# Shorter lags between the stages of an edge stream, other route bounds, and a later load of the second expert

## What is computed

```
hn  = layernorm(x)
z   = hn @ W_func.T ;  h_s = hn @ W_self.T
e   = leaky_relu([z[src], z[dst], edge_attr] @ W_att.T)
a   = softmax of e over the edges of one target
x   = x + hn + relu(h_s + segment_sum(a * z[src], dst))     # hn where a node has no edge
y   = layernorm(x)
p   = softmax(y @ router_w.T);  keep the 2 largest of 8, scaled to sum 1
out = x + sum over the two experts of p_e * (silu(y @ w1_e.T) * (y @ w3_e.T)) @ w2_e.T
```

## Time and profile before

| | us |
|---|---|
| median of 3 runs | 1053.97 |
| the three runs | 1053.77 to 1055.1 |
| the profiled execution, its own time | 1052.19 |
| its span, from the first to the last instruction | 1050.0 |
| PE busy / DVE / POOL / ACT in the span | 849.4 / 635.3 / 590.1 / 449.5 |
| gathers of the stream, first and last start | 51.6 and 573.7 |
| marker behind the last logits | 621.92 |

### The profile page before, as it was taken

How to read it: one execution, slowest core, us unless ns; L and a number is a source line. 1 busy time by engine, 2 the same in 40 slices (tenths; PEclk the granted TensorE clock), 3 DMA queues, 4 the chain that set the end, 5 groups by cost and what they waited for, 6 DMA issues and landing times.

```text
span 1050.0 us, 19071 instructions
## 1 busy us (share of the span) xinstructions
PE 849.4 (81%) x4512; PEld 707.3 (67%) x4513; DVE 635.3 (61%) x2235; ACT 449.5 (43%) x1066; POOL 590.1 (56%) x554
## 2 busy tenths in 40 slices
PE   6954888964776777677577968999999999999995
PEld 6811444654664566465456856998988989898994
DVE  6624555565655677766677858556556555656553
ACT  4422233454556546545645861343424333342331
POOL 1077777777777777777776003635455353535332
PEclk9986998988888789788878979999999999999998
DMA  7676576556555455555555243544243522222221
GB/s 235 209 229 207 179 214 183 142 138 220 137 146 143 134 147 138 139 146 135 143 148 135 68 130 129 126 83 101 58 109 60 111 34 41 36 40 35 41 41 20
DMA packets 81158, 128.86 MB, mean 123 GB/s; under 512 B 21373, under 2 KB 56706, under 8 KB 80594
## 3 DMA queue, kind: packets, MB, share of 16 engines
q0 software_dynamic: 30720, 69.90, 28.6%
q1 hardware_dynamic: 43161, 51.59, 16.1%
q10 hardware_dynamic: 7200, 6.56, 1.9%
HBM read 106.86 MB, written 17.86 MB: 119 GB/s over the span
## 4 chain that ended last, share of the span: by engine, by line
PE 56%; DVE 12%; issue 10%; DMA 9%; POOL 7%; DVEq 3%; ACT 1%; POOLq 0%; SPq 0%; ACTq 0%
PE bank L1439 17%; PE bank L1373 13%; DMA early<-ztab,early 7%; PE bank L1480 7%; POOL early L828 7%; PE bank L1334 3%; PE bank L1487 3%; PE bank L1468 3%; PE bank L1160 2%; DVE acc L1906 2%; PE bank L1176 1%; PE bank L1245 1%; PE bank L1242 1%; PE bank L1213 1%; DVE early L1849 1%
## 5 line engine op out<-in xcount | busy, mean ns | idle before, releaser
L828 POOL DMA_INDIRECT early<-ztab,early x416 | 396.7, 954 | 174.6 <-issue 171.8
L1439 PE MATMUL bank<-split_w,operands 128*128 x1344 | 235.4, 324 | 3.8 <-issue 2.7
L1373 PE MATMUL bank<-early,W 128*128 128x258 f32 x832 | 231.7, 430 | 4.9 <-DVE W L1883 4.6
L1439 PEld LDWEIGHTS bank<-split_w,operands 128*128 128x128 f32 x1344 | 211.0, 189 | 9.1 <-issue 7.6
L1373 PEld LDWEIGHTS bank<-early,W 128*128 128x128 f32 x832 | 170.7, 215 | 53.1 <-issue 23.2
L875 POOL DMA_INDIRECT xg<-ttab,slot_rows x56 | 58.3, 1040 | 235.5 <-DVE late L2075 163.7
L1049 ACT ACTIVATE W<-early 128x128 f32<-128x128 f32 x208 | 91.0, 484 | 124.5 <-PE bank L1373 121.3
L1334 PE MATMUL bank<-ident,early 128*16 128x128 f32 x104 | 24.4, 382 | 137.5 <-DVE early L1866 137.4
L868 POOL DMA_INDIRECT out_rows<-late,slot_rows x56 | 103.1, 1841 | 36.6 <-issue 15.4
L1129 ACT ACTIVATE late<-bank 128x384 f32<-128x384 f32 x56 | 27.4, 490 | 198.7 <-PE bank L1439 193.7
L1334 PEld LDWEIGHTS bank<-ident,early 128*16 128x16 f32 x104 | 10.4, 121 | 149.5 <-DVE early L1866 146.8
(11 more groups left out here) (243 smaller groups left out, 1415.6 us busy)
## 6 DMA issues: line engine op xcount, KB each, us to landing
W<-in_wt SPq DMA_DIRECT2D x26, 512.0 KB, 4.5
W<-in_experts SPq DMA_DIRECT2D x40, 266.5 KB, 2.8
early<-ztab,early POOLq DMA_INDIRECT x416, 2.9
W<-in_experts SPq DMA_DIRECT2D x3, 2132.0 KB, 9.0
early<-in_x SPq DMA_DIRECT2D x26, 128.0 KB, 2.2
early<-ztab SPq DMA_DIRECT2D x25, 128.0 KB
early<-late SPq DMA_DIRECT2D x25, 128.0 KB
out_rows<-early ACTq DMA_DIRECT2D x25, 128.0 KB, 2.1
```

The costliest lines, as they stand in the source:

```text
L828: nc.gpsimd.indirect_dma_start(out=zg[:, k * KG + c, :], out_offset=None, in_=ztab, in_offset=bass.IndirectOffsetOnAxis(ap=src_here[:, k / ...
L1373: last = mm(ps[2 + k // 2 % 2][:, 0:ZR], prob_hot[:, k % 3, c * P:(c + 1) * P], zg[:, k * KG + c, :], start=(k % 2 == 0 and c == 0), stop= ...
L1439: last = mm(bank[:, 0:n], x[:, (k % 2 * KC + c) * P:(k % 2 * KC + c + 1) * P], split_w[:, bass.ds(at + (part + w + c * H), n)], start=(i = ...
```

## The change

The lags of the lists are made smaller and the stages inside a step stand in another order. Sums (`weighted`) go from lag 8 to 6, `spread` from 7 to 6, `exps`, `largest` and `shifted_down` from 7 to 5, `runs` and `runs_T` from 5 to 4, `back_copy`, `mirror_back` and `distance` from 6 to 5, `add_sums` from 9 to 7. A tile's path starts at lag 18 instead of 21 (`settled_den`) and ends at lag 25 instead of 34 (`logit_copy` and the routes). `node_load` goes from lag 25 to 18 on SP. The waits that guard shared banks follow (`BEHIND`, `hi + 6`, `ROUTES[b][1] + 6`), as do the steps in which PE runs filler products (`BUSY_FROM`). The middle route takes 9 tiles and the last one 8. SP waits for the marker instead of the last sums before it loads expert 1.

```
-BEHIND = SETTLED // BATCH + 2
+BEHIND = SETTLED // BATCH + 1
-ROUTES = ((0, 8), (8, 16), (16, TILES))
+ROUTES = ((0, 8), (8, 17), (17, TILES))
...
-                                                 (SETTLED + 13, tiled(node_load))])
-                sp.wait_ge(sums_added, GROUPS // 2)
-                sp.wait_ge(next_added, GROUPS // 2)
+                                                 (SETTLED + 6, tiled(node_load))])
+                sp.wait_ge(stream_over, 1)
                 expert_load(1)
...
-                run(act, GROUPS, AHEAD, PEEL, [(7, exps), (7, spread), (6, back_copy), (6, distance), (0, later_scores),
+                run(act, GROUPS, AHEAD, PEEL, [(5, back_copy), (SETTLED + 11, tiled(std2)), (SETTLED + 7, tiled(share_of)),
...
-                run(pe, GROUPS, AHEAD, PEEL, [(4, score_rows_of), (8, weighted), (6, mirror_back),
+                run(pe, GROUPS, AHEAD, PEEL, [(5, mirror_back), (SETTLED + 12, tiled(hn2_T)),
+                                              (6, weighted), (SETTLED + 7, tiled(share_behind)),
...
-                run(dve, GROUPS, AHEAD, PEEL, [(5, runs), (7, largest), (0, plus_s1), (7, shifted_down), (9, add_sums),
+                run(dve, GROUPS, AHEAD, PEEL, [(6, spread_rest), (SETTLED + 13, tiled(logit_copy)), (0, plus_s1),
```

More of the change, by code:

```diff
@@ L83 @@
 EXPERTS_AFTER = (44,)
-BUSY_FROM, BUSY_TO = GROUPS - SETTLED - 7, GROUPS - SETTLED + 2
+BUSY_FROM, BUSY_TO = GROUPS - SETTLED - 6, GROUPS - SETTLED + 2
 LAST_AT = BATCH * (TILES - 2) + 1
@@ L1355, in mirror_back @@
                     for b, (lo, hi) in enumerate(ROUTES[:-1]):
-                        if batch(k, r) == hi + 8:
+                        if batch(k, r) == hi + 6:
                             pe.wait_ge(choice_ready, 3 * b + 3)
@@ L1818, in later_scores @@
                     for part in range(1, len(PARTS)):
-                        if isinstance(t, int) and t == COPY_AT[part] + 3:
+                        if isinstance(t, int) and t == COPY_AT[part] + 2:
                             scores_kept(part)
@@ L1915, in settled_den @@
                     den_of(j, k, r)
-                run(dve, GROUPS, AHEAD, PEEL, [(5, runs), (7, largest), (0, plus_s1), (7, shifted_down), (9, add_sums),
-                                               (0, s2_at), (SETTLED + 9, tiled(settled_den)),
-                                               (SETTLED + 14, tiled(where_edge)), (0, s2_sum),
-                                               (SETTLED + 13, tiled(x_plus_hn)), (SETTLED + 14, tiled(residual)),
-                                               (0, plus_s2), (SETTLED + 15, tiled(stats2)), (SETTLED + 17, tiled(inv_std2)),
-                                               (0, leaky), (SETTLED + 15, tiled(mean_var2)),
-                                               (SETTLED + 17, tiled(neg_mean2)), (SETTLED + 22, tiled(logit_copy)),
-                                               (7, spread_rest), (0, later_scores), (SETTLED + 22, route)])
+                run(dve, GROUPS, AHEAD, PEEL, [(6, spread_rest), (SETTLED + 13, tiled(logit_copy)), (0, plus_s1),
+                                               (5, largest), (7, add_sums), (0, s2_at), (5, shifted_down),
+                                               (SETTLED + 6, tiled(settled_den)), (SETTLED + 10, tiled(where_edge)),
+                                               (SETTLED + 11, tiled(inv_std2)), (0, s2_sum), (SETTLED + 8, tiled(x_plus_hn)),
+                                               (SETTLED + 10, tiled(residual)), (SETTLED + 11, tiled(neg_mean2)),
+                                               (0, plus_s2), (SETTLED + 10, tiled(stats2)), (0, leaky),
+                                               (SETTLED + 10, tiled(mean_var2)), (4, runs), (0, later_scores),
+                                               (SETTLED + 13, route)])
                 v.memset(tick[:, :], 0.0).then_inc(stream_over, 1)
```

16 lines of the change are left out of this document (7 added, 9 removed).

## The result

The changed kernel takes 1064.37 us (median of 4 runs, 1062.32 to 1066.92) beside 1054.53 for the kernel before: a ratio of 1.0101, 95% interval 1.0087 to 1.0115. It is slower by about 1%, and the forecast of 1052.6 with its range up to 1056.0 was wrong. Its profiled execution took 1064.42 us with a span of 1062.3, that is 12.3 over the span of before.

A forecast was written before the change was run, and what follows sets the result against it. The prediction took POOL's gather issues to bound the stream, followed by a drain to the marker. Marker 0.4 us earlier and 1.0 less behind it sum to -1.4, on the median 1053.97: 1052.6, range 1048.5 to 1056.0.

The forecast's parts named there:

- The stream: The 104 groups of gathers: POOL waits for nobody, 5.03 us a group, so shorter lags gain and cost nothing there.
- the slower rival: PE at half clock through most of the drain, marker behind 624, kernel over 2.1 us slower; chance 0.13.
- starving ring: Rival in the stream: waits within longer steps starve the ring and POOL stalls, +5 us, 1058; chance 0.04.
- The drain: From the stream's end to the marker: marker at 617.9 at full clock, 4.0 us below 621.92.
- link (a): Drain's start: group 103's score, sums of 98, score rows to 584.5, then scan and one-hots of 99 to 587.5.
- the three of the prediction: Places in the drain where PE is mostly idle: 584.5 to 587.5, 593.2 to 595.3 and 603.8 to 609.
- link (d): Drain's end: tiles 22 to 24 in turn through one bank, from 603.8 to 617.9.
- Link (b): Drain after 587.5: sums of 99, tile 21, statistics, root, one-hots of 101 to 595.3; PE hole of 2.2 us.
- PE's clock: In the drain: two falls to half clock, +1.0 and +2.6 us, moving the marker from 617.9 to 621.5.
- Group 103: The last group, at the drain's start: VectorE takes it up at 578.4, 1.2 us late (bounds 0 and 2.2).
- The table of the exponential: ACT's table load in the drain, between back-copy and exponential: 1.28 us, ends before it matters, adds 0.
- Behind the marker: Last route has 16 pairs of one-hots instead of 18 and fewer columns: -1.0 us; expert 1's later load adds 0.

The follow-up runs named there:

- e6: Kernel before with only the routes' split changed, to 8, 9 and 8 tiles: 1055.13 us, ratio 1.0001.
- e10: Kernel before with 8 filler matmuls a step instead of 2 in its last steps: 1056.38 us, ratio 1.0013.
- e4: Changed kernel with VectorE's one-hots of groups written as scalar_tensor_tensor instead of tensor_scalar, order as it is: 1073.05 us, ratio 1.0176.
- e1: Changed kernel with VectorE's one-hots of groups moved to mid-step, behind add_sums: 1096.76 us, ratio 1.0425.
- e13: e9 with further PE fillers ahead of the two clock falls still left in the drain: 1052.72 us, ratio 0.9993.
- e5: Changed kernel with VectorE's scan moved on into the next step, behind the one-hots and the logits' copy: 1057.4 us, ratio 1.0024.
- e14: e13 with 3 instead of 8 fillers a step in the last steps: 1053.28 us, ratio 0.9992.
- e7: e5 plus filler matmuls on PE in the drain, no list changed: 1055.21 us, ratio 1.0000.
- e2: Changed kernel with VectorE's one-hots of groups back ahead of the scan, lag 5 for 6: 1055.76 us, ratio 1.0021.
- e3: Kernel before with VectorE's one-hots of groups moved directly behind the scan, lag 8 for 7: 1069.52 us, ratio 1.0155.
- e8: e5 with ScalarE's one-hots of groups ahead of the tile's root, share and idle: 1056.09 us, ratio 1.0007.
- e9: e5 with both ScalarE's one-hots ahead of the root and the PE fillers in the drain: 1054.31 us, ratio 0.9992.
- e11: Changed kernel with VectorE's one-hots of groups using two fixed numbers instead of per-partition scalars: 1063.9 us (2 runs), ratio 1.009.
- e12: Changed kernel with the scan replaced by one tensor_tensor maximum of the same operands: 1055.62 us, ratio 1.0018.

## Why the prediction was wrong, step by step

**The stream: wrong, and this is the step that failed.** "So the stream of 104 groups lasts as long as POOL issues, 5.03 us a group, and the change leaves POOL's order alone." POOL's order is left alone, and the stream does last as long as POOL issues; but that is 5.13 us a group now, for a gather's own duration is not fixed. I took 1.26 us from issue to issue for a property of POOL, asked only whom POOL waits for the earlier trace rows, and priced the reordering of VectorE's list at 0. A wait that lies inside an instruction is shown by no row of waits; it is shown by that instruction's longest duration. The fault can be named more narrowly: I followed what waits on VectorE's moved one-hots ("sums behind VectorE's one-hots of the same step"), and not what they stand next to. The order of the two lists showed the new neighbours. The size: 9.5 us in the profiles; by the ratios 1.0101 - 1.0024 is about 8 us. (In e6 and e10, whose lists are those of before, the last gather starts at 575.4 and 575.2, so some 1.5 us of such a difference can be scatter.) Of the signs that were named, the first one caught it, the last gather at 573.7. The sign of the slower rival, a marker behind 624, came too, and misled: most of the marker's lateness was there before the drain began.

A page of the Trainium skill speaks to it that I didn't weigh: "SBUF — State Buffer", section "Who interferes with whom". It says that VectorE and GpSimd share one pair of ports, that GpSimd needs it to generate the descriptors of its own DMAs, and that a VectorE instruction in a two-port mode, which tensor_scalar can enter, blocks GpSimd for the whole of it where it issues first. The trace agrees in kind: nine gathers of 1.65 to 2.08 us beside such instructions. It differs in the condition. The same tensor_scalar apart from the scan (80 times in that stream) never has a gather of over 1.18 us beside it, and the other form, with two tensors as its inputs, which by the page interferes with an instruction of GpSimd that reads, holds the gathers at least as long (e4). By that rule alone, without what stands ahead of the one-hots, the kernel before would hold gathers too: its 95 pairs of one-hots in the stream have no gather over 1.09 beside them.

**No wait of POOL, no starving ring: right** in the changed kernel (its gaps are 0.30 throughout). e1 shows what the rival would have looked like.

**The drain: partly right in form, too short in size.** At full clock the sum ran from the last gather at 573.7 to 617.9, 44.2 us. e13, at full clock but with fillers in PE's way, took 48.7. How long the drain is at full clock without them no run shows. Up to the end of tile 22's products the sum gave 30.1 from the last gather's start (573.7 to 603.8) and e13 needs 32.4 (575.10 to 607.55). In link (a) I let PE have the sums of 98 as soon as their one-hots are there, and overlooked the sums of 97 ahead of them: in e5 PE stands still for 2.72 us, a hole that isn't among the three of the prediction, runs the sums of 97 at half clock (3.58) and comes to those of 98 9.2 us behind the last gather, for the 7.0 of the sum. The score rows end 12.4 behind it, for 10.8. In link (d), 14.1 of the sum, e13 needs 16.3 and e14, with fewer late fillers, 15.2. Link (b) was right: its hole of PE, predicted at 2.2, is 2.34, behind the predicted chain of root, share, idle, one-hots:

```profile
605.62 0.29 ACT L966 ACTIVATE early<-early,eps 128x1 f32<-128x1 f32 x1 [2.43 <-DVE early L1644]
...
606.62 0.86 ACT L1048 ACTIVATE W<-early 128x128 f32<-128x128 f32 x2
...
607.53 2.72 PE L1371 MATMUL bank<-early,W 128*128 128x258 f32 x7 [2.34 <-ACT W L1048]
```

**PE's clock: the right worry, set too low.** Two falls for 3.6 us were forecast. The changed kernel's windows show it below full speed in most of the drain:

```profile
595.00:600.00 5.00, 2.93 (x11) 2.36 (x12) 2.12 (x6) 2.91 (x7) 0.00 (x0) 0.80 0.00 0
605.00:610.00 5.00, 2.66 (x8) 2.03 (x8) 1.47 (x7) 3.71 (x10) 0.00 (x0) 0.82 0.29 89
620.00:625.00 5.00, 4.07 (x18) 3.23 (x19) 0.66 (x3) 2.06 (x6) 0.00 (x0) 0.69 0.15 52
630.00:635.00 5.00, 3.39 (x18) 2.39 (x18) 1.44 (x9) 3.56 (x6) 0.00 (x0) 0.71 0.24 80
```

From 595 to 635 the windows lie between 0.69 and 1.00; in the drain before they were at 1.00 up to the fall at 618. e7 prices it: about 2.5 us, just clear of the intervals. The slower rival, half clock through most of the drain, names a part of the loss, but not the larger one. The page that the prediction set beside it, "TensorE: Matmul & The Clock Gate" of the Trainium skill, section "HAM oscillation — how this bites in real kernels", tells of matmuls that run at the low level again and again behind waits. The traces agree: behind a hole of 2.72 eight sum rows take 3.58 us in e5, and with that hole filled 1.98 in e13.

**Group 103:** predicted 4.7 us after the last gather's start. It was 5.6 in the changed kernel and 4.7 in e5 (580.46). Right to within a microsecond, once the stream is set aside (5.4 in e13).

**The table of the exponential:** predicted 0. The exponential starts 0.01 to 0.02 behind the load's end, as in the earlier trace rows; VectorE does wait for it, 1.98 us once, but PE has other sums in that time. Right for what the runs can tell.

**Behind the marker:** predicted -1.0, found -0.4 in the profiles, and e6, the routes alone, gives no gain that can be measured. Expert 1 is as predicted: its conversions begin 8.4 us behind the marker (9.4 predicted), and the copy of the tokens stands at 650.45, 15.8 behind it (15.4 predicted), waiting for PE and not for the conversions:

```profile
643.08 3.85 ACT L549 ACTIVATE split_w<-W 128x2842 fp32r<-128x2842 f32 x2 [3.82 <-DMA W<-in_experts]
650.45 0.38 ACT L1004 ACTIVATE acc<-bank 100x256 f16<-100x256 f32 x1 [3.53 <-PE bank L1295]
```

**The sum of it.** Predicted -1.4, by the median of the runs about +10. Of this the pair of scan and one-hots is about 8 us (shown by e2, e5 and, the other way round, e3). The other 2.5 are the drain: PE's holes and the half clock behind them. Fillers alone give them back (e7); ScalarE's one-hots ahead of the root gain 1.8 (e8), which isn't clear of noise. In no run do the shorter lags themselves gain anything measurable in the drain: with these losses taken away (e9, e13) the kernel is level with the kernel before. As e13's fillers cost PE time of their own, a gain without them isn't excluded.

## What to carry to other kernels

An engine that waits for nobody is still not independent: before a reordering is priced at nothing, look at the longest duration of the bounding instruction as well as at its waits, and at what the moved instructions will stand next to on a neighbouring engine. Bringing stages closer together took slack out of this pipeline's end, but also work that had kept PE busy and its clock up. And a stage is best kept out of a list position where it waits for another engine's late result while a third engine waits for what is queued behind it.

## What the runs showed of the hardware that was not expected

A gather issued by POOL is stretched from 0.95 to as much as 2.3 us when VectorE runs a scan (16 x 512, 1.21 us) and, directly behind it, one-hots (128 x 128, two of them). For so long a hold it takes both: one-hots apart from the scan leave a gather at up to 1.21 us (e5; 1.39 in the other form of e4), and a tensor_tensor behind the scan leaves it at up to 1.1. Neither another form of the one-hots (e4) nor fixed scalars (e11) take it away. With a tensor_tensor of 0.68 us in the scan's place (e12) the hold is still there and shorter, 1.31 at most. And a hold isn't bound to the scan: the stream's first gather took up to 1.57 us (e13; 1.51 in e2) beside a burst of VectorE's casts and tensor_scalars with no scan in it.

When the gather begins decides how long it gets, for those that are held have a common end. Seven of the nine long gathers of the changed kernel end 2.13 to 2.14 us behind the scan's start, wherever they began (0.28 to 0.49 behind it), which is just when VectorE's burst ends (2.08 to 2.09); the two whose burst lacked the copy of the logits end at 2.34 and 2.35, as do 18 of the 20 in e3, whose bursts lack it too, and in e4 all that are held at the pairs end at 2.53 to 2.54. For these later ends I have no explanation. One-hots of the routes directly behind a scan did it too (1.80 us in e1, 1.65 in e4, 2.00 in e11). Why an instruction of this length ahead of the one-hots matters stays open.
